# Row sums moved to POOL in wide pieces, and copies, a row maximum and exponentials placed earlier at the round changes

## What is computed

```python
k = x_in @ wk + bk;  v = x_in @ wv + bv          # x_in: normalised context
slots = q_mu + jnp.exp(q_logsig) * noise         # noise: normalised x
for _ in range(T):                               # T = 3
    prev = slots
    q = _ln(slots, lnq_g, lnq_b) @ wq + bq
    attn = jax.nn.softmax(jnp.einsum('bnd,bkd->bnk', k, q) / scale, axis=-1) + EPS_ATTN
    attn = attn / jnp.sum(attn, axis=1, keepdims=True)
    slots = jnp.einsum('bnk,bnd->bkd', attn, v) @ wu + bu + prev
    h = _ln(slots, lnm_g, lnm_b) @ w1 + b1
    slots = jax.nn.gelu(h, approximate=False) @ w2 + b2 + slots
    slots = _ln(slots + x_cls[:, None, :], lnp_g, lnp_b)
x = x + slots
x = x + ffn(layernorm(x))                        # gelu, layernorm, two ternary products
```

## Time and profile before

| what | value |
|---|---|
| time, median of 3 runs | 330.23 us (330.23 to 330.33) |
| the profiled execution's own time | 329.51 us |
| its span, first to last instruction | 327.6 us |
| PE, DVE, ACT, POOL busy | 313.2, 278.0, 227.8, 216.5 us |
| mean granted TensorE clock | 1.000 of full |

### The profile page before, as it was taken

The page is one execution under the profiler, slowest core; times in us unless marked ns, Lnnn a source line. Parts: engine busy times, 40 slices in busy tenths (PEclk is TensorE's granted clock), DMA queues, the critical chain, the costliest instruction groups (busy, mean ns, idle before and its releaser), DMA issues. The chain is left out here.

```text
span 327.6 us, 6157 instructions
## 1 busy us (share of the span) xinstructions
PE 313.2 (96%) x1758; PEld 259.5 (79%) x1758; DVE 278.0 (85%) x816; ACT 227.8 (70%) x504; POOL 216.5 (66%) x417
## 2 busy tenths in 40 slices
PE   8899999999999989999999889899998889999985
PEld 8788887888888878888888777688875657777764
DVE  3699976989899899998998999988797998888763
ACT  2378985967576968776768675677556868777771
POOL 3169967245679867557798564677989688856331
PEclk9999999999999999999999999999999999999999
DMA  7999000000000000000000000000000000000001
GB/s 280 327 296 395 23 1 0 0 2 0 1 3 0 1 3 0 2 1 1 0 2 0 1 2 1 1 3 0 2 0 0 2 34 34 33 32 28 7 34 64
DMA packets 5312, 13.24 MB, mean 40 GB/s; under 512 B 672, under 2 KB 672, under 8 KB 4896
## 3 DMA queue, kind: packets, MB, share of 16 engines
q1 hardware_dynamic: 4160, 10.88, 9.2%
q10 hardware_dynamic: 1120, 1.98, 1.6%
HBM read 10.76 MB, written 2.10 MB: 39 GB/s over the span
## 5 line engine op out<-in xcount | busy, mean ns | idle before, releaser
L288 DVE BATCH_NORM_STATS2 stats<-S 128x6 f32<-128x256 f32 x112 | 42.1, 416 | 9.0 <-DMA S<-ctx 3.6
L339 PE MATMUL ps_mid<-XT,KT 128*128 128x256 f32 x192 | 46.0, 383 | 3.4 <-ACT XT L355 3.4
L339 PE MATMUL ps_low<-V,PR 128*128 128x257 f32 x192 | 46.1, 382 | 0.9 <-DVE PR L886 0.6
L339 PE MATMUL ps_mid<-XT,wt 128*128 128x256 f32 x192 | 45.6, 380 | 0.8 <-ACT XT L355 0.7
L339 PE MATMUL ps_low<-wn,GT 128*128 128x256 f32 x192 | 45.4, 379 | 0.0
L339 PEld LDWEIGHTS ps_low<-V,PR 128*128 128x128 f32 x192 | 36.1, 190 | 7.4 <-DVE PR L886 2.5
L339 PEld LDWEIGHTS ps_mid<-XT,KT 128*128 128x128 f32 x192 | 34.6, 190 | 8.5 <-ACT XT L355 4.8
L306 POOL TENSOR_TENSOR lnm_ab<-lnm_mv,mhalf 128x2 f32<-128x2 f32 x24 | 17.3, 720 | 35.7 <-DVE lnm_mv L296 35.7
L339 PEld LDWEIGHTS ps_low<-wn,GT 128*128 128x128 f32 x192 | 36.3, 190 | 5.0
L339 PEld LDWEIGHTS ps_mid<-XT,wt 128*128 128x128 f32 x192 | 34.7, 190 | 5.1 <-ACT XT L355 1.2
L355 ACT ACTIVATE XT<-ps_t 128x512 f32<-128x512 f32 x56 | 33.0, 589 | 7.8 <-PE ps_t L331 7.8
(11 more groups left out here) (127 smaller groups left out, 708.0 us busy)
## 6 DMA issues: line engine op xcount, KB each, us to landing
S<-ctx SPq DMA_DIRECT2D x8, 256.0 KB, 3.8
X<-x SPq DMA_DIRECT2D x8, 256.0 KB, 3.6
out<-X SPq DMA_DIRECT2D x8, 256.0 KB, 2.0
rowv<-rows SPq DMA_DIRECT2D x1, 1920.0 KB, 10.6
wf<-w_fc_t SPq DMA_DIRECT2D x1, 1024.0 KB, 11.4
wf<-w_proj_t SPq DMA_DIRECT2D x1, 1024.0 KB, 13.6
wt<-w_tr ACTq DMA_DIRECT2D x1, 512.0 KB, 4.4
wn<-w_nat ACTq DMA_DIRECT2D x1, 512.0 KB, 5.6
```

Of the source, the lines that this page charges most:

```text
L288: dve.bn_stats(ln.st[:, at, j, 0:6], tiles[:, j]).then_inc(ln.stats_done, 1)
L339: last = pe.matmul(dst(m), lhs_t[:, c, m * P:(m + 1) * P], rhs[:, c, 0:n], start=(c == 0), stop=(c == 1))
```

## The change

The `b2` sums and the `lnp_b` sums both go to POOL, into round one's first steps, as instructions of 128x512 (an item of X at a time, or two condition rows at a time; the row operand is repeated by a broadcast). DVE's `shift_x` is dropped. POOL's L481 waits for item b's one sum, and the waits for the condition rows move to where these are used. At the round changes the place of `scale_p`, of the query norm's apply and of one row maximum is changed.

```diff
+            def shift_rows(s):
+                if s == 0:
+                    pool.wait_ge(rows_in, 16)
+                for k in ((0, 1), (2, 3), (4,), (5,), (6,), (7,))[s]:
+                    pool.tensor_tensor(X[:, k], X[:, k], both_rows(row("lnp_b")), ALU.add).then_inc(x_shifted, 1)
+                if s in range(1, 1 + B // 2):
+                    two = slice(2 * s - 2, 2 * s)
+                    pool.tensor_tensor(cond_row[:, two], cond_row[:, two], both_rows(row("b2")), ALU.add)\
+                        .then_inc(c_ready, 1)
...
             def rounds(t, s, last):
-                if s == 2 and t == 0 and not last:
-
-                    pool.wait_ge(rows_in, 16)
-                    for b in range(B):
-                        pool.tensor_tensor(cond_row[:, b], cond_row[:, b], row("b2"), ALU.add).then_inc(c_ready, 1)
-                    pool.wait_ge(c_ready, B)
+                if s < 6 and t == 0 and not last:
+                    shift_rows(s)
                 if t == 0 and not last and s < 2:
                     ln_coef(pool, lni, B - 2 + s, s)
...
                         if last:
-                            pool.wait_ge(x_shifted, J2 * b + J2)
+                            pool.wait_ge(x_shifted, b + 1)
...
                     if half == 0:
+                        pool.wait_ge(c_ready, b // 2 + 1)
                         pool.wait_ge(xm_ready, r * B + (b + 1))
...
             def apply_norms(t, s, last):
-                if s in (STEPS + 2, STEPS + 3):
-                    s = {STEPS + 2: -1, STEPS + 3: -1 if last else STEPS + 2}[s]
+                if last and s >= STEPS + 2:
+                    return
+                if not last and s in (STEPS + 1, STEPS + 2, STEPS + 3):
+                    s = {STEPS + 1: -1, STEPS + 2: STEPS + 1, STEPS + 3: STEPS + 2}[s]
...
                     copy_xt(act, ring(r, half, b), b % 2)
+                if s == STEPS + 2 and not last:
+                    apply_norms(t, s, last)
...
+                third = not last and s == STEPS + 3
+                if not third:
+                    apply_q()
                 mid = item(t, s, 1, last)
-                read_first = last or (mid and mid[1] == 1) or s in (STEPS + 1, STEPS + 2)
+                read_first = last or (mid and mid[1] == 1) or s in (STEPS + 1, STEPS + 2, STEPS + 3)
...
-                if read_first:
+                if third:
+                    apply_q()
+                if read_first and (last or s != STEPS + 2):
                     apply_norms(t, s, last)
...
-            def shift_x(b):
-                for j in range(J2):
-                    dve.tensor_tensor(X[:, b, j], X[:, b, j], row("lnp_b"), ALU.add).then_inc(x_shifted, 1)
...
+                third = not last and s == STEPS + 3
+                if third:
+                    row_max(mid)
...
-                if mid and mid[1] == 0 and not (change or behind):
+                if mid and mid[1] == 0 and not (change or behind or third):
                     row_max(mid)
...
-                if t == ROUNDS - 2 and s >= STEPS + 2 and not last:
-                    shift_x(s - STEPS - 2)
```

More of the change, by code:

```diff
@@ L116, in row, with both_rows @@
             return rowv[:, ROW[name]:ROW[name] + D]
+        def both_rows(r):
+            return r[:, None, :].broadcast_to([P, J2, D])
         def col(name, c):
@@ L641, in rounds, with apply_q @@
                                    accum_out=absum[:, k:k + 1]).then_inc(mag_ready, 1)
[L642 to L645, removed]
+                def apply_q():
+                    if it := item(t, s, -Q_APPLY, last):
+                        r, half, b = it
+                        if half == 0 and s + Q_APPLY >= STEPS:
+                            ln_apply(act, lnq, (r - 1) * B + b, b, Y[:, b], XH[:, b], xq_ready)
+                third = not last and s == STEPS + 3
+                if not third:
+                    apply_q()
                 mid = item(t, s, 1, last)
-                read_first = last or (mid and mid[1] == 1) or s in (STEPS + 1, STEPS + 2)
+                read_first = last or (mid and mid[1] == 1) or s in (STEPS + 1, STEPS + 2, STEPS + 3)
                 if not read_first:
@@ L856, in into_ffn @@
             def into_ffn(s):
[L857 to L860, removed]
                 if s in (STEPS - 4, STEPS - 3):
```

## The result

The changed kernel takes **331.52 us** (median of 13 runs, 329.85 to 332.64) against 330.33 (13 runs, 329.70 to 331.02) of the kernel before beside it: a ratio of 1.0032, 95% interval 1.0021 to 1.0044. It is slower, by 0.3 to 0.7 %. The forecast was 330.6 and its range, 329.0 to 332.3, holds the time; yet the sum behind it lacks a term of 1.5 to 2.8 us, and a smaller one of 0.6 goes the other way.

The account below looks back on a forecast made before the run. TensorE, busy 96 % of the span, was taken as the bound. Head +3.1, first round change +0.15 and second -2.85 summed to +0.4 on the median 330.23: 330.6 us, range 329.0 to 332.3.

Parts of the forecast that it names:

- What bounds the kernel: Whole kernel: TensorE, busy 96 % of the span; a delay at the head reaches the first round change undiminished.
- POOL at the head: Round one's first steps: wide sums ahead of norm factors start item 0's attention product 3.2 later, net +3.1.
- the five pieces: POOL's wide sums of steps 0 and 1, ahead of item 7's norm factors, at 1.22 each.
- the 1.35 that the text names as a sign of being wrong: POOL: the forecast would be wrong if one wide sum took over 1.35.
- The step that failed: Head: behind its wait TensorE takes 0.05 to start and 1.83 for a product.
- The text's own mark for an error: Head: wrong if the first `ps_low` product stood before 57.5 or after 59.8; forecast 58.79.
- Does DVE keep up?: Head: DVE's two scalings of item 0 each wait for a POOL piece of 1.22, hidden by 0.6.
- Change 1: First round change: TensorE's wait moves from step 19 to step 22; 0.79 gained is gone, net +0.15.
- Change 2: Second round change: without DVE's sums of x and with the new order, step 27's transposes come 2.85 earlier.
- Behind step 27 both kernels have the same work: After the second change, to the end: same work, which TensorE starts 2.85 earlier.
- The sum: Whole kernel: +3.1 + 0.15 - 2.85 = +0.4, giving 330.6.
- the dearer head: Rival, head: a piece with a broadcast operand takes 1.42, item 7's factors come 1.0 later; 331.6, chance 0.24.

Follow-up runs that it names:

- e5: Changed kernel with POOL's twelve wide sums spread, one a step, behind that step's norm factors; 326.61 us against 329.59, ratio 0.9900.
- e8: Changed kernel with 7 matmuls that nobody reads put into TensorE's head wait; 330.51 us against 329.59, ratio 1.0026.
- e9: The changed kernel measured and profiled once more, nothing altered, in a later batch; 331.75 us against 329.56, ratio 1.0074.
- e1: Changed kernel with POOL's five wide sums of steps 0 and 1 behind item 7's norm factors; 331.04 us against 330.38, ratio 1.0039.
- e3: Changed kernel with ACT's and DVE's order at the round changes put back as before; 331.05 us against 330.38, ratio 1.0010.
- e6: As e5, but with the old order of ACT and DVE at the round changes; 326.34 us, ratio 0.9893.
- e11: As e6, plus one POOL wait putting DVE first in the feed-forward loop at every item but the first; 325.64 us against 330.21, ratio 0.9863.
- e2: Kernel before with only the new order of ACT and DVE at the round changes; 331.27 us against 330.38, ratio 1.0032.
- e12: As e8, plus one POOL wait putting DVE first in the feed-forward loop at every item but the first; 329.54 us, ratio 0.9983.

## Why the prediction was right or wrong

- **What bounds the kernel**: right. What TensorE lost at the head of the changed kernel came out at step 19 undiminished; of what it gained there in e5, about half did.
- **POOL at the head**: right in its mechanism, and closer than it deserves. The factors were ready at 54.41 for 54.37, TensorE's product started at 56.97 for 56.96 (58.79 less 1.83), and with the clock held up the first `ps_low` product at 58.89 for 58.79. But the five pieces took 6.37 from start to start (2.64 and 3.73 by the rows above), not 6.10, and what hides that is luck: POOL began on them at 45.74, not at 46.03. One of them, the first, has a span of 1.45, over the 1.35 that the text names as a sign of being wrong. By step 19 the head costs +3.2 (e8) for +3.1, and +3.4 counted from the first logits product.
- **The step that failed** is the one behind that wait: "TensorE takes 0.05 to start and 1.83 for a product behind a wait". That was read from the 1.99 of a product behind a wait of 0.99; no wait of 3.4 is in the trace of before, where the longest of TensorE's is 1.3. Behind this one the product took 3.58 and the next up to 2.84: +1.5 in one profile, +2.8 in the other (step 19 in e9 and in the changed kernel against e8, counted from the first logits product). No term, no rival and no bound stood for it. The text's own mark for an error, a first `ps_low` product behind 59.8, was passed: 60.55.
- **"Does DVE keep up?"**: right where it was asked, the scaling of item 0 took 1.63 and was hidden. It was only asked there: the scaling of W1, ahead of it on DVE, took 2.35 where the trace of before has 1.39; that was hidden too, behind the wait. e1 shows what it costs once that wait is gone.
- **Change 1**: right, +0.11 for +0.15, with the two waits at the steps named (0.19 and 0.51).
- **Change 2**: right in size, -2.9 in the eight other profiles of the table that have the new order and POOL's sums (-3.15 in the first one) for -2.85. The working took the order to be part of it; e3, e6 and e11 have the old order and give -3.0, so the new order wins nothing there and costs about the 0.1 that it costs at change 1.
- **"Behind step 27 both kernels have the same work"**: wrong by -0.6. Two waits at the start of the feed-forward part are shorter in the changed kernel, and within 0.02 of its values in every other without DVE's sums of x. The kernel before, then the changed one:

```profile
259.59 1.16 PE L1094 MATMUL ps_mid<-ident,KT 128*128 128x128 f32 x8 [0.93 <-DVE V L810]
...
265.01 1.16 PE L1094 MATMUL ps_mid<-ident,KT 128*128 128x128 f32 x8 [0.78 <-DVE V L810]
```

```profile
262.30 1.16 PE L1109 MATMUL ps_mid<-ident,KT 128*128 128x128 f32 x8 [0.71 <-DVE V L832]
...
267.37 1.16 PE L1109 MATMUL ps_mid<-ident,KT 128*128 128x128 f32 x8 [0.43 <-DVE V L832]
```

  Why is not settled; it goes with the sums (e3 has it, e2 has not), not with the order. The other thing in that stage is the order of DVE and POOL at one item, 0.6 to 0.75.
- **The sum**: +3.2 + 0.1 - 2.9 - 0.6 is -0.2, where +0.4 was forecast, and -0.2 is what the profile of e12 has by its span (327.4 for 327.6); the clock adds 1.5 to 2.8 in the two profiles, and 0, 1.9 or 3.3 by the executions of e3. The two misses partly cancel: that the range held is in part luck. Of the rivals the dearer head has the sign and nearly the time, 331.6, but for another reason than the one it names.

What stays open: why the same kernel is 0.3 % slower than the one before in one batch of runs and 0.7 % in another. The kernel before itself has medians from 329.56 to 330.38 in the batches on record, and two that differ by 0.8 carry the same chip number.

## What to carry to other kernels

A wait of the engine that bounds the kernel is not only its length: look whether the trace has one that long, and if it has none, put a price on a lower clock behind it. Work that is moved to POOL is not idle filler where DVE scales, casts or adds in SBUF beside it: one long piece holds each such DVE instruction up to its own end, so put pieces where DVE reads PSUM, takes statistics or waits. And when DVE and POOL can hold each other up and become ready at the same moment, say in the program who is first.

## What the runs showed of the hardware

- The granted clock was 0.50 behind a wait of 3.36 and behind one of 3.70 (e1), and stayed at 1.000 where 7 matmuls filled the same stretch. Behind the same wait of 3.36 one execution had one slow product, another two (e9 and the first profile); twelve executions of one kernel (e3) fall into three groups by their mean clock, 1.9 and 3.3 us apart from the fastest.
- A cast of 128x8 takes 0.16 where POOL stands still (e5) and 1.16 beside back-to-back pieces of POOL (e1). Statistics of 128x256 take 0.74 for two, beside such pieces or not.
- Of DVE's product and POOL's sum that meet in the feed-forward loop, one runs at its own length and the other is held up: 1.28 and 2.21 where DVE's row starts 0.2 earlier, 2.37 and 1.27 where it starts 0.02 earlier (e5). Which of the two was issued first the profile does not show.
